# A stack of four graph layers on one core: two PSUM banks in turn for the attention passes' extra sums, and another order of VectorE's work in a step

## The chip, the cores and the metric

The kernel runs on one NeuronCore of a Trainium2 chip. The metric is device time in microseconds (us) of one execution, lower being better. The engines are TensorE (PE), VectorE (DVE), ScalarE (ACT), GpSimd (POOL) and SyncE (SP). Each has its own queue of instructions and works through it in order; they meet at semaphores.

## The reference

There are 3125 nodes with 128 features and 53125 edges, sorted by target node. Four layers are added to x, each on relu(layernorm(x)): a graph attention layer (one head), a relational layer, two graph convolutions with norms, and two transformer convolutions (four heads), the second on the first one's result. The change concerns the attention layers, which are segment softmaxes followed by weighted sums:

```
alpha = sum_d q[dst] * (k[src] + e) / sqrt(C)         # per edge and head
amax  = segment_max(alpha, dst);  p = exp(alpha - amax[dst])
denom = segment_sum(p, dst);      w = p / denom[dst]
out   = segment_sum((v[src] + e) * w, dst) + x @ Ws + bs
```

The kernel divides at the end. So it needs for every node the sum of p times v (the main sums, 128 features) and a few extra sums: of p and of p times the edge weight for each head (8 rows in the transformer layers), and 3 rows in the first layer.

## The kernel before, in words

There are three attention passes, all written by the same Python functions: the first (k = 0) for the graph attention layer, and the second and third (k = 1 and 2, called L3 in the code) for the transformer convolutions. Edges go in tiles of 128, groups of four tiles (512 edges), and chunks of eight groups. A pass has 13 chunks, so 104 groups, and every engine runs a loop over steps s that is unrolled, one group per step and stage:

- POOL gathers the source rows of group s with four indirect DMAs (`attention_gathers`, L518, the gathers are L532) into a ring. The ring has 24 slots in the first pass and 15 in the others. A slot is free once the messages of its old group are made, so POOL waits for `msg_ready`.
- SP loads the query windows of the targets (L436) and the targets' places (L424).
- PE expands the query windows to edges (bank QX, `expand`), and 12 groups later (LAG) sums messages per node (`node_sums`, L1512): it clears bank NU[s % 2] with a matmul of zeros, adds four tiles of messages times one-hot, then clears MTB in the same way and adds four tiles of edge factors times one-hot. It waits for `ex_used` before it clears MTB, which is to say until DVE has taken the previous group's extra sums out of this one bank.
- DVE multiplies queries by keys (`products`), sums by head (`head_sums`, L981), finds the running maximum by scans once in a chunk, scales values to messages (`messages`), and adds PE's sums from PSUM to the sums in SBUF (`add_sums`, L985). Elementwise adds and products of two tensors all show as line L834, a helper.
- ACT makes the one-hot matrices and the exponentials.

The order in a DVE step of the second and third pass is: head sums of s-1, main sums of s-13, extra sums of s-13, first half of messages of s-11, products of s, a part of the chunk's score work (`FIRST`), second half of the messages, another part of the score work (`SECOND`). The first pass has no head sums and no products, and makes its messages in one piece (four instructions, L1008). With r the step's place in its chunk, the score work is at r = 0 (scores, then scans, which need PE's transpose in bank MID), r = 1 (scans over tiles, segment maxima), r = 2 (below the maximum, change of maximum, factors), and r = 4 (the shared node's sums are rescaled with `facs`, L1091 and L1092). PE's own part of it (`turn_scores`, `tile_ends`, `tile_starts`, `turn_maxima`, `spread_changes`, all in bank MID) stands after its `node_sums` at r = 0, 1 and 2. ACT reads columns of MID for `facs` and then signals `fac_ready`.

## Time and profile before

| what | value |
|---|---|
| median of three runs | 4391.96 us (4387.48 to 4392.62) |
| the profiled execution's own time | 4389.91 us |
| its span from first to last instruction | 4387.9 us |
| busy: PE, DVE, ACT, POOL | 2793.6, 2080.7, 1555.9, 2371.9 us |
| first attention pass | from about 250 to 885 us |
| second and third pass | about 2910 to 3550 and 3700 to 4350 us |
| mean granted TensorE clock | 0.772 |

No engine is busy for more than 64% of the span. "Idle before" in a row is the time in which the engine stood still just before the instruction, and the name behind the arrow is what ended it. "Remote" means that a semaphore ended it that the profile can't put down to an instruction that had just finished. A line is often a helper's, so groups are told apart by the names of their tiles: `sums_transposed<-sums_transposed,NU` is the main sum, `extra_sums_transposed<-extra_sums_transposed,MTB` the extra sum, `MTB<-start_penalty,zero_weights` the clearing matmul of the extra sums' bank.

### The profile page before, as it was taken

The numbers are of one execution on the slowest core, as the hardware profiler recorded it, in microseconds if no ns is written. First come the engines' busy times: TensorE is split into PE (matmuls) and PEld (weight loads), VectorE is DVE, ScalarE is ACT, GpSimd is POOL, SyncE is SP. The second block draws the span as 40 slices with busy tenths as digits, with TensorE's granted clock in tenths as the row PEclk, the third lists the DMA queues.
The fourth block names the chain that finished last, engine by engine and source line by source line (L and its number), as shares of the span: only waits on it lengthen the run. The fifth ranks groups of instructions, "written<-read, shape, count | busy, mean of one in ns | idle before, by whom it ended". The sixth has DMA issues, their size and how long they took to land.

```text
span 4387.9 us, 52346 instructions
## 1 busy us (share of the span) xinstructions
PE 2793.6 (64%) x15364; PEld 2036.7 (46%) x15364; DVE 2080.7 (47%) x4427; ACT 1555.9 (35%) x3919; POOL 2371.9 (54%) x2449
## 2 busy tenths in 40 slices
PE   3177788872333356877767877557676774666667
PEld 2055556632222334555534554345555553455555
DVE  5033334641222345566546655235555663555557
ACT  2054444540000033333343333234454423444443
POOL 1745555116666636666366664335666534555653
PEclk9976666885555668899879988567888886887887
DMA  4322222131111112222122221345555424455541
GB/s 86 68 56 59 62 60 62 23 130 47 46 46 48 45 56 53 53 53 53 53 61 55 53 52 34 105 126 141 139 144 146 129 81 128 135 139 135 146 135 45
DMA packets 351656, 360.74 MB, mean 82 GB/s; under 512 B 125198, under 2 KB 274389, under 8 KB 351381
## 3 DMA queue, kind: packets, MB, share of 16 engines
q0 software_dynamic: 89600, 211.77, 18.4%
q1 hardware_dynamic: 255638, 143.69, 12.7%
q10 hardware_dynamic: 6148, 1.93, 0.3%
q8 instruction: 139, 2.28, 0.2%
q14 instruction: 131, 1.07, 0.1%
HBM read 327.08 MB, written 30.26 MB: 81 GB/s over the span
## 4 chain that ended last, share of the span: by engine, by line
PE 41%; another core or an unknown queue 21%; DVE 15%; issue 15%; ACT 3%; POOL 1%; DMA 1%; SPq 1%; DVEq 1%; ACTq 1%; POOLq 0%
PE QX L1368 20%; PE NU L1368 12%; PE MTB L1368 7%; DVE sums_transposed L834 3%; DVE extra_sums_transposed L834 2%; DVE gathered_rows L834 1%; DVE messages L834 1%; DVE query_key_products L834 1%; POOL gathered_rows L549 1%; PE MID L1368 1%; SPq L436 1%; DVE scan_scores L981 1%; ACT window_distance L698 1%; ACTq L601 0%
## 5 line engine op out<-in xcount | busy, mean ns | idle before, releaser
L532 POOL DMA_INDIRECT gathered_rows<-key_value_rows,src_index x832 | 829.6, 997 | 646.2 <-DVE messages L834 356.3
L834 DVE TENSOR_TENSOR sums_transposed<-sums_transposed,NU 128x512 f32 x624 | 425.7, 682 | 1140.7 <-remote 740.6
L549 POOL DMA_INDIRECT gathered_rows<-gcn_rows,src_index x720 | 684.5, 951 | 470.0 <-issue 194.6
L532 POOL DMA_INDIRECT gathered_rows<-gat_rows,src_index x416 | 397.0, 954 | 391.6 <-DVE messages L1008 191.1
L1368 PE MATMUL NU<-start_penalty,zero_weights 128*128 128x512 bf16 x624 | 278.5, 446 | 423.1 <-DVE sums_transposed L834 328.1
L549 POOL DMA_INDIRECT gathered_rows<-relation_rows,src_relation_index x416 | 400.9, 964 | 206.2 <-issue 123.8
L794 ACT ACTIVATE gathered_rows<-iota_window,dst_in_window_by_edge 128x128 f32<-128x128 f32 x832 | 265.1, 389 | 608.4 <-remote 445.0
L729 ACT ACTIVATE edge_node_onehot<-iota_window,dst_in_window_by_edge 128x128 f32<-128x128 f32 x1248 | 394.8, 387 | 155.1 <-remote 135.4
L1368 PEld LDWEIGHTS NU<-edge_node_onehot,messages 128*128 128x128 f32 x2496 | 414.0, 234 | 47.0 <-issue 26.5
L1368 PE MATMUL NU<-gathered_rows 128*128 128x128 f32 x2496 | 395.5, 310 | 56.5 <-issue 33.3
L1368 PE MATMUL NU<-edge_node_onehot,messages 128*128 128x128 f32 x2496 | 413.6, 318 | 24.7 <-issue 24.6
L1368 PEld LDWEIGHTS NU<-gathered_rows 128*128 128x128 f32 x2496 | 386.7, 224 | 85.7 <-issue 66.0
L1368 PE MATMUL MTB<-edge_node_onehot,edge_factors 128*8 128x128 f32 (+1 forms) x2496 | 412.8, 321 | 0.0
L1368 PE MATMUL QX<-query_window,gathered_rows 128*128 128x384 bf16 x1120 | 248.9, 368 | 156.1 <-DVE gathered_rows L834 79.7
L1368 PE MATMUL QX<-query_window,node_edge_onehot 128*128 128x132 f32 (+1 forms) x1248 | 213.3, 313 | 191.7 <-issue 95.8
L834 DVE TENSOR_TENSOR extra_sums_transposed<-extra_sums_transposed,MTB 8x512 f32 (+1 forms) x312 | 210.0, 673 | 256.8 <-remote 183.0
L1368 PEld LDWEIGHTS MTB<-edge_node_onehot,edge_factors 128*8 128x8 f32 (+1 forms) x2496 | 256.1, 103 | 132.1 <-issue 33.5
L698 ACT ACTIVATE window_distance<-dst_in_window_row,minus_partition 128x512 bf16<-128x512 bf16 x312 | 224.2, 718 | 237.9 <-issue 140.4
L1368 PE MATMUL MTB<-start_penalty,zero_weights 128*8 128x512 bf16 x312 | 142.1, 455 | 249.1 <-DVE extra_sums_transposed L834 232.8
L1368 PEld LDWEIGHTS NU<-start_penalty,zero_weights 128*128 128x128 bf16 x624 | 78.4, 126 | 461.3 <-DVE sums_transposed L834 344.9
L709 ACT COPY query_edge_term<-QX 128x16 f32<-128x16 f32 x208 | 38.0, 183 | 717.6 <-DVE query_key_products L834 613.8
L1368 PEld LDWEIGHTS QX<-query_window,node_edge_onehot 128*128 128x128 f32 x1248 | 188.3, 230 | 223.9 <-issue 216.2
(294 smaller groups left out, 4357.0 us busy)
## 6 DMA issues: line engine op xcount, KB each, us to landing
query_window<-query_rows SPq DMA_DIRECT2D x832, 66.0 KB
dst_in_window_row<-dst_in_window SPq DMA_DIRECT2D x156, 256.0 KB
gathered_rows<-key_value_rows,src_index POOLq DMA_INDIRECT x832
relation_rows<-gathered_rows SPq DMA_DIRECT2D x25, 512.0 KB
gathered_rows<-gcn_rows,src_index POOLq DMA_INDIRECT x720
dst_in_window_row<-src_place_and_block SPq DMA_DIRECT2D x28, 256.0 KB
gathered_rows<-gat_rows,src_index POOLq DMA_INDIRECT x416
query_window<-gat_target_scores SPq DMA_DIRECT2D x416, 2.0 KB
```

The lines of the kernel that those rows point to most:

```text
L436: sp.dma_start(qwin[:, s % QS, t, 0:a["ww"]].bitcast(u8), win[ds(bases[t], P * row)].rearrange("(p w) -> p w", w=row)).then_inc(qwin_in[s ...
L532: pool.indirect_dma_start(out=rows_of(a, s)[:, t, :], out_offset=None, in_=a["table"], in_offset=bass.IndirectOffsetOnAxis(ap=srcI[:, TPG ...
L549: pool.indirect_dma_start(out=linear_rows(p["k"], k)[:, t, :], out_offset=None, in_=p["table"], in_offset=bass.IndirectOffsetOnAxis(ap=p[" ...
L698: own.step(act.activation(STa[:, s % 2, :], drow_sb[:, half, q:q + TPG * P], ACT.Square, bias=neg_iota_p[:]))
L709: act.copy(qwe[:, s // GPC % 2, :, TPG * g:TPG * (g + 1)].rearrange("p h t -> p t h"), QX[s % 2][:, :, D:D + HEADS]).then_inc(S["qwe_kept" ...
L729: last = act.activation(to[:, t, :], iota_j[:], ACT.Square, bias=dstP[:, TPG * s + t:TPG * s + t + 1], scale=-1.0)
L794: last = act.activation(to[:, t, :], iota_j[:], ACT.Square, bias=dstP[:, TPG * k + t:TPG * k + t + 1], scale=-1.0)
L834: return dve.tensor_tensor(o, x, y, op)
L981: d.step(dve.tensor_reduce(alphax[:, :, TPG * g:TPG * g + TPG].rearrange("p h t -> p t h"), prod[:, s % 2, :].rearrange("p (t h d) -> p t ...
L1368: return pe.matmul(o, l, r, start=start, stop=stop)
```

## The change

Extra sums go to two PSUM banks. In the first pass they alternate between MTB and the free upper half of QX0. In the other two passes they go to MID where r is 3, 5 or 7, and to MTB where r is 0, 1, 2, 4 or 6. MID is also the bank of the score work, so PE waits for `fac_ready` before it clears MID for extra sums, and `turn_scores` waits until the last extra sums in MID are taken. PE's wait for `ex_used` before it clears a bank now names the last group that used this bank. DVE's extra sums are a function of their own (`add_extras`), called after the second half of the messages and before `SECOND`. The main sums wait for the previous main sums (`nu_used`), and PE waits for `nu_used` before it clears NU. No arithmetic, no transfer and no count of instructions on an engine changes.

```diff
--- before.py
+++ after.py
@@ -334,6 +334,18 @@
         att_base = lambda a: a["k"] * NG
         last_step = NG + LAG + 2
 
+        def ext_bank(k, s):
+
+            if k == 0:
+                return QXf[0][:, 512:1024] if s % 2 else MTB[:]
+            return MID[:] if (s + LAG) % GPC in (3, 5, 7) else MTB[:]
+
+        def ext_before(k, s):
+
+            same = [q for q in range(s) if (s % 2 == q % 2 if k == 0 else
+                                            ((s + LAG) % GPC in (3, 5, 7)) == ((q + LAG) % GPC in (3, 5, 7)))]
+            return same[-1] if same else None
+
         def in_slot(s, ring_size):
             return s // ring_size + 1
 
@@ -990,11 +1002,17 @@
                     dve.wait_ge(S["nu_ready"], b + s + 1)
                     if s % GPC == 0:
                         dve.wait_ge(S["rescaled"], cb + s // GPC + 1)
-                    elif not L3 or s + LAG >= NG:
+                    else:
+                        dve.wait_ge(S["nu_used"], b + s)
+                    tt(numS[:, w], numS[:, w], NU[s % 2][:], ALU.add).then_inc(S["nu_used"], 1)
+
+                def add_extras(s):
+
+                    w = ds(held["base"][s % 4], SPAN)
+                    dve.wait_ge(S["ex_ready"], b + s + 1)
+                    if s:
                         dve.wait_ge(S["ex_used"], b + s)
-                    tt(numS[:, w], numS[:, w], NU[s % 2][:], ALU.add).then_inc(S["nu_used"], 1)
-                    dve.wait_ge(S["ex_ready"], b + s + 1)
-                    tt(extS[0:ex, w], extS[0:ex, w], MTB[0:ex, 0:SPAN], ALU.add).then_inc(S["ex_used"], 1)
+                    tt(extS[0:ex, w], extS[0:ex, w], ext_bank(k, s)[0:ex, 0:SPAN], ALU.add).then_inc(S["ex_used"], 1)
 
                 def messages(s, t0, t1):
                     g = s % GPC
@@ -1107,6 +1125,8 @@
                         FIRST[r](c)
                     if 0 <= s + 1 - LAG < NG:
                         messages(s + 1 - LAG, TPG // 2 if L3 else 0, TPG)
+                    if 0 <= s - 1 - LAG < NG:
+                        add_extras(s - 1 - LAG)
                     if r in SECOND and 0 <= c < NCH:
                         SECOND[r](c)
                 dve.wait_ge(S["ex_used"], b + NG)
@@ -1485,6 +1505,8 @@
                     last.then_inc(S["expand_done"], 1)
 
                 def turn_scores(c):
+                    if L3 and c:
+                        pe.wait_ge(S["ex_used"], b + GPC * c + GPC - LAG)
                     pe.wait_ge(S["alpha_ready"], cb + c + 1)
                     x = (alpha if L3 else alphax)[:].rearrange("p h t -> p (h t)")
                     pe.transpose(MID[:, 0:P], x, I[:]).then_inc(S["xT_ready"], 1)
@@ -1515,15 +1537,20 @@
                     off = offsets(s, f"off_{k}")
                     pe.wait_ge(S["s_ready"], sb0 + s + 1)
                     pe.wait_ge(S["msg_ready"], b + s + 1)
+                    if s >= 2:
+                        pe.wait_ge(S["nu_used"], b + s - 1)
                     clear(NU[s % 2], P)
                     for t in range(TPG):
                         last = mm(NU[s % 2][:, ds(off[t], P)], msg[:, s % 2, t, :], Sb[:, s % SBN, t, :], False, t == TPG - 1)
                     last.then_inc(S["nu_ready"], 1)
-                    if s:
-                        pe.wait_ge(S["ex_used"], b + s)
-                    clear(MTB, 8)
+                    to, before = ext_bank(k, s), ext_before(k, s)
+                    if before is not None:
+                        pe.wait_ge(S["ex_used"], b + before + 1)
+                    if L3 and (s + LAG) % GPC in (3, 5, 7):
+                        pe.wait_ge(S["fac_ready"], cb + min((s + LAG) // GPC, NCH))
+                    clear(to, 8)
                     for t in range(TPG):
-                        last = mm(MTB[0:ex, ds(off[t], P)], pe8[:, c % 2, 0:ex, TPG * g + t], Sb[:, s % SBN, t, :], False, t == TPG - 1)
+                        last = mm(to[0:ex, ds(off[t], P)], pe8[:, c % 2, 0:ex, TPG * g + t], Sb[:, s % SBN, t, :], False, t == TPG - 1)
                     last.then_inc(S["ex_ready"], 1)
 
                 HOPS = {0: (turn_scores, tile_ends), 1: (tile_starts, turn_maxima), 2: (spread_changes,)}
```

DVE, second pass, one step with nothing of the score work (r = 3), before:

```order
L981 TENSOR_REDUCE scan_scores<-query_key_products 128x4x4 [waits k_used]
L834 ISA [waits nu_ready]
L834 TENSOR_TENSOR sums_transposed<-sums_transposed,NU 128x512
L834 REGISTER_ALU [waits ex_ready]
L834 TENSOR_TENSOR extra_sums_transposed<-extra_sums_transposed,MTB 8x512
L834 TENSOR_TENSOR messages<-gathered_rows,edge_factors 128x256
L834 TENSOR_TENSOR query_key_products<-QX,gathered_rows 128x512 [waits gathered13,expand_done]
L834 TENSOR_TENSOR messages<-gathered_rows,edge_factors 128x256
```

The same step of DVE with the change (the helper's line is now L846):

```order
L993 TENSOR_REDUCE scan_scores<-query_key_products 128x4x4 [waits k_used]
L846 ISA [waits nu_used,nu_ready]
L846 TENSOR_TENSOR sums_transposed<-sums_transposed,NU 128x512
L846 TENSOR_TENSOR messages<-gathered_rows,edge_factors 128x256
L846 TENSOR_TENSOR query_key_products<-QX,gathered_rows 128x512 [waits gathered13,expand_done]
L846 TENSOR_TENSOR messages<-gathered_rows,edge_factors 128x256
L846 REGISTER_ALU [waits ex_used,ex_ready]
L846 TENSOR_TENSOR extra_sums_transposed<-extra_sums_transposed,MID 8x512
```

The extra sums and their wait for `ex_ready` have moved behind both halves of the messages and the products.

PE, second pass, the end of one step's main sums and the extra sums behind them, then the chunk's transpose of scores, before:

```order
L1368 MATMUL NU<-edge_node_onehot,messages 128x128
L1368 MATMUL MTB<-start_penalty,zero_weights 8x512 [waits ex_used]
...
L1368 MATMUL NU<-start_penalty,zero_weights 128x512 [waits msg_ready,s_ready]
...
L1368 MATMUL MTB<-start_penalty,zero_weights 8x512 [waits ex_used]
...
L1490 MATMUL MID<-identity,scores 128x128 [waits alpha_ready]
```

The same place of PE with the change (helper's line L1388):

```order
L1388 MATMUL NU<-edge_node_onehot,messages 128x128
L1388 MATMUL MID<-start_penalty,zero_weights 8x512 [waits fac_ready,ex_used]
...
L1388 MATMUL NU<-start_penalty,zero_weights 128x512 [waits nu_used,msg_ready,s_ready]
...
L1388 MATMUL MTB<-start_penalty,zero_weights 8x512 [waits ex_used]
...
L1512 MATMUL MID<-identity,scores 128x128 [waits alpha_ready,ex_used]
```

PE's instructions stand in the same order; every second bank of extra sums is now another one, and the waits name other groups.

## Rows read from the trace of the kernel before

**Rows 1.** Windows: stretch, us, busy (count) per engine, clock, DMA share, GB/s

```profile
250.00:885.00 635.00, 521.79 (x2768) 387.76 (x2768) 274.81 (x892) 310.14 (x731) 302.69 (x319) 0.69 0.26 54
2910.00:3550.00 640.00, 456.29 (x2818) 355.61 (x2819) 372.77 (x858) 319.05 (x834) 356.91 (x356) 0.81 0.47 130
3700.00:4350.00 650.00, 446.12 (x2784) 347.32 (x2784) 370.23 (x847) 317.32 (x831) 359.18 (x356) 0.82 0.47 128
```

**Rows 2.** Waits of POOL in passes one, two, three: us, times, longest

```profile
POOL gathered_rows L532 <- DVE messages L1008: 159.0, 45, 6.1
...
POOL gathered_rows L532 <- DVE messages L834: 134.0, 43, 5.9
...
POOL gathered_rows L532 <- DVE messages L834: 142.0, 36, 7.6
```

**Rows 3.** Groups (lines view), the extra sums on DVE, passes one to three

```profile
L834 DVE TENSOR_TENSOR extra_sums_transposed<-extra_sums_transposed,MTB 3x512 f32 x104 | 70.1, 674 | 134.8 <-remote 91.4 <-PE MTB L1368 43.0
...
L834 DVE TENSOR_TENSOR extra_sums_transposed<-extra_sums_transposed,MTB 8x512 f32 x104 | 69.9, 672 | 53.9 <-remote 42.8 <-PE MTB L1368 6.6 <-issue 4.2
...
L834 DVE TENSOR_TENSOR extra_sums_transposed<-extra_sums_transposed,MTB 8x512 f32 x104 | 69.9, 673 | 68.2 <-remote 48.8 <-issue 9.9 <-PE MTB L1368 9.1
```

**Rows 4.** Groups (lines view), PE clearing the bank of extra sums, passes one to three

```profile
L1368 PE MATMUL MTB<-start_penalty,zero_weights 128*8 128x512 bf16 x104 | 53.7, 516 | 63.5 <-DVE extra_sums_transposed L834 63.5
...
L1368 PE MATMUL MTB<-start_penalty,zero_weights 128*8 128x512 bf16 x104 | 44.3, 426 | 99.1 <-DVE extra_sums_transposed L834 91.6 <-issue 7.5
...
L1368 PE MATMUL MTB<-start_penalty,zero_weights 128*8 128x512 bf16 x104 | 44.0, 423 | 86.4 <-DVE extra_sums_transposed L834 77.7 <-issue 8.7
```

**Rows 5.** Timeline, second pass: start us, us, engine, what, [idle before]

```profile
3099.93 1.05 PE L1368 MATMUL NU<-edge_node_onehot,messages 128*128 128x128 f32 x8
...
3106.36 0.94 POOL L532 DMA_INDIRECT gathered_rows<-key_value_rows,src_index  x1 [0.30 <-issue]
3109.43 0.69 DVE L834 TENSOR_TENSOR sums_transposed<-sums_transposed,NU 128x512 f32 x1 [8.92 <-remote]
3110.03 0.67 DVE L834 TENSOR_TENSOR extra_sums_transposed<-extra_sums_transposed,MTB 8x512 f32 x1
...
3112.08 0.42 DVE L834 TENSOR_TENSOR messages<-gathered_rows,edge_factors 128x256 f32<-128x256 f32 x1
...
3112.77 0.94 POOL L532 DMA_INDIRECT gathered_rows<-key_value_rows,src_index  x1 [5.46 <-DVE messages L834]
```

**Rows 6.** Timeline, second pass, half a chunk later

```profile
3140.85 0.95 POOL L532 DMA_INDIRECT gathered_rows<-key_value_rows,src_index  x1 [0.30 <-issue]
3142.89 0.68 DVE L834 TENSOR_TENSOR extra_sums_transposed<-extra_sums_transposed,MTB 8x512 f32 x1 [2.88 <-remote]
...
3145.10 0.94 POOL L532 DMA_INDIRECT gathered_rows<-key_value_rows,src_index  x1 [3.30 <-DVE messages L834]
```

**Rows 7.** Timeline, first pass

```profile
525.85 0.94 POOL L532 DMA_INDIRECT gathered_rows<-gat_rows,src_index  x1 [0.30 <-issue]
...
528.47 0.68 DVE L834 TENSOR_TENSOR extra_sums_transposed<-extra_sums_transposed,MTB 3x512 f32 x1 [3.60 <-remote]
...
530.19 0.94 POOL L532 DMA_INDIRECT gathered_rows<-gat_rows,src_index  x1 [3.40 <-DVE messages L1008]
```

**Rows 8.** Timeline, second pass, the chunk step with the change of maximum

```profile
3123.25 0.67 DVE L834 TENSOR_TENSOR extra_sums_transposed<-extra_sums_transposed,MTB 8x512 f32 x1
...
3124.47 0.38 PE L1368 MATMUL MTB<-start_penalty,zero_weights 128*8 128x512 bf16 x1
...
3125.56 0.41 DVE L834 TENSOR_TENSOR messages<-gathered_rows,edge_factors 128x256 f32<-128x256 f32 x1
...
3126.55 0.14 ACT L719 ACTIVATE rescale_factors<-MID 8x1 f32<-8x1 f32 x1
...
3128.75 0.38 PE L1368 MATMUL MTB<-start_penalty,zero_weights 128*8 128x512 bf16 x1 [0.40 <-issue]
...
3130.49 0.67 DVE L834 TENSOR_TENSOR sums_transposed<-sums_transposed,NU 128x512 f32 x1
```

## The prediction

> **What bounds the kernel now.** I began with the waits of each engine, went on to the windows of the three attention passes, then to the groups of lines inside them, and last to the timeline of single steps.
>
> The windows say how much of the kernel the change can touch. The passes take 635, 640 and 650 us, together 1925 us, or 6.11, 6.15 and 6.25 us for each of 104 groups. Nothing else is edited. In none of them is an engine busy all the time, PE being nearest with 522 of 635 us in the first pass [rows 1].
>
> The nearest thing to a floor is POOL. Each group costs it four gathers, and in a run of gathers one row reads 0.94 us with 0.30 us of idle time before it [rows 5]. Four times 1.24 us is 4.96 us a group, 516 us a pass. What POOL takes beyond that is mostly time in which it waits for a ring slot, that is for DVE's messages: 159.0, 134.0 and 142.0 us, in 45, 43 and 36 waits [rows 2]. These 435.0 us in 124 waits are what can be won in all. A faster PE or DVE helps only so far as it shortens them.
>
> The timeline shows what such a wait is made of. DVE stands still for 8.92 us before a main sum. PE's matmuls for that sum ended at 3100.98, but DVE goes on only at 3109.43, 2.1 us after POOL's last gather ended at 3107.30. POOL stood because its ring was full. Then DVE takes its main sum, the extra sum and the messages, and POOL starts again at 3112.77, after 5.46 us [rows 5]. So DVE's long stops do not end when PE is done. They end when the stream of gathers pauses, and the ring is refilled only when DVE has reached the end of the messages.
>
> Two spots have a second stop between the main sum and the extra sum. DVE has the rows and factors for the next messages, but the extra sum stands ahead of them in its queue and waits for PE's result: 2.88 us in one spot [rows 6] and 3.60 us in another [rows 7].
>
> **Part 1: the extra sum leaves the way to the messages.** The extra sum begins 0.60 us after the main sum, which is listed with 0.69 us, and is listed itself with 0.67 us [rows 5]. Adds of this size follow each other 0.60 us apart, so that is what one of them costs. With the change it stands behind the messages. In each of POOL's 124 waits for messages the slot is free 0.60 us sooner: 124 x 0.60 = 74 us.
>
> **Part 2: the stop before the extra sum leaves the way to the messages too.** DVE stood 134.8, 53.9 and 68.2 us before extra sums, 256.9 us in all [rows 3]. Not all of it cost POOL anything, since it was still gathering in part of it. In one spot the last gather ended at 3141.80 and the extra sum began at 3142.89, so POOL stood in 1.09 of 2.88 us [rows 6]. In the other it ended at 526.79 and the extra sum began at 528.47: 1.68 of 3.60 us [rows 7]. Together that is 2.77 of 6.48 us, or 43%. Taken over all, 0.43 x 256.9 = 110 us.
>
> **Part 3: the second bank.** PE stood 63.5, 91.6 and 77.7 us before it could clear the bank of extra sums, because DVE had not taken the last ones [rows 4]. With two banks it clears the other one and goes on to the next query windows and main sums. I cost this at nothing in the sum: in rows 5 PE had ended long before DVE was let go. It does keep part 2 from coming back, because a delayed extra sum no longer holds PE. Without it, moving the extra sums later would hold PE longer.
>
> **Part 4: what is given back.** No work disappears. DVE does the same 0.60 us in the same step, and the stop before the extra sum moves behind the messages, where it holds up the next step. Also, POOL now goes on gathering where it used to pause. By rows 5 to 7 a stop of DVE lasts until the gathers pause, so a stop that used to end at 3142.89 will now last through four more gathers, some 5 us, before POOL runs out of slots. Then there is one pause for the two that there were, with its own restart. The bounds are that all comes back (0) or nothing does (74 + 110 = 184 us). I see no row that puts it nearer to one end, because the restart itself (main sum, messages) stays, while the number of restarts should fall. I take half, 92 us.
>
> A rule speaks for the upper end. "SBUF — State Buffer" of the Trainium skill, under "Who interferes with whom", says that DMA never contends with a compute engine and that PE never waits on anyone. By that, the stops that end as the gathers pause are coincidence, nothing would be given back, and the sum would be the full 184 us. The three stops in rows 5 to 7, ending 2.1, 1.1 and 1.7 us after the last gather, speak against it.
>
> **Part 5: the new waits.** The waits for `nu_used` name sums that were done a step earlier in the same queue, so they cost nothing. The wait for `fac_ready` at r = 3 has room: ACT's last factor is done at 3126.69, and PE clears its bank for the next extra sums at 3128.75 [rows 8], 2.1 us later. At r = 1 and r = 2 the banks do not alternate in the second and third pass. There PE waits for an extra sum that has moved behind the products, the score work and the messages. In rows 8 it would end about where the messages end, at 3125.97, and PE cleared the bank at 3124.47. So PE is 1.5 us late once in a chunk. Its main sums were then needed about 2 us after they were ready (the extra sum's bank is cleared at 3128.75, right behind them, and DVE takes the main sum at 3130.49), so this is hidden. Without that slack it costs 1.5 us x 26 chunks = 39 us.
>
> **Sum.** 4389.9 - 92 = 4298 us for the profiled execution. The median of the runs is 2 us above that execution, so I say 4300 us.
>
> **Rivals.**
>
> *All is given back.* The stop only changes its place, POOL pauses as long in all as before, and the time stays at 4392, within 9 us. For it speaks that the sum over a chunk of what DVE must do is unchanged and that its stops follow the gathers. Against it speaks that POOL has more slots open when DVE stops. Chance 0.12.
>
> *Nothing is given back.* 4390 - 184 = 4206, with the median 4208 us. This is what the rule named above would make of it. Chance 0.15. It would show as stops of DVE that end with PE's matmuls.
>
> *Slower: PE's late extra sums at r = 1 and 2 become the bound.* The place is PE's queue in the second and third pass. It is in order, so a bank cleared late delays the change of maximum, the next query windows and the next main sums behind it. The price is 1.5 us for each of 26 chunks, or 39 us. Where POOL's longer stream also draws out DVE's stops so that parts 1 and 2 come to nothing, the time is 4392 + 39 = 4431 us. It decides once PE's lead over DVE falls under 1.5 us at r = 3; in rows 8 it is about 2. Chance 0.16.
>
> *The change doesn't do what it says* can be left out: the order of the two queues shows the move, and there is no scheduler between.
>
> **How the numbers follow.** The forecast (half kept) has 0.57, full gain 0.15, no change 0.12, slower 0.16. About 0.2%, 9 us, is what a measurement of this kernel can tell from no change. Faster is 0.57 + 0.15 = 0.72, the same 0.12, slower 0.16. The range takes in the forecast, most of the full gain and the unchanged time: 4215 to 4400 us. Left out are the slower case and a little of the far end. The likeliest case alone would be 4240 to 4360 us.
>
> **What would show it.** If the steps are right, POOL's waits for messages in the three passes fall from 435 us to about 340, and in number below 124. PE's waits of 233 us before clearing a bank of extra sums fall to under 100. DVE's idle time moves from before the extra sums to before the main sums, and some stops grow longer than the 8.92 us of rows 5. The passes together take about 1830 us instead of 1925, and nothing changes outside them. Part 4 is wrong if DVE's stops end with PE's matmuls; part 5 is wrong if DVE begins to wait for PE's main sums or factors at r = 3 or 4. The prediction fails as a whole if POOL waits as long as before.

## Result and profile after

| | before | changed |
|---|---|---|
| median of four runs each, same chip | 4390.61 us (4387.48 to 4392.62) | 4439.74 us (4433.54 to 4442.13) |
| profiled execution, its span | 4389.91, 4387.9 us | 4438.21, 4436.2 us |
| busy: PE, DVE, ACT, POOL | 2793.6, 2080.7, 1555.9, 2371.9 us | 2779.1, 2072.8, 1558.2, 2334.9 us |

The ratio is 1.0124, 95% interval 1.0104 to 1.0143: 49 us slower, where 92 us less was forecast. No engine does more work, so the 49 us are waits.

The three passes in the windows of the changed kernel (us, then busy time and count of PE, PEld, DVE, ACT, POOL, clock, DMA share, GB/s):

```profile
250.00:885.00 635.00, 489.94 (x2774) 366.98 (x2775) 272.04 (x893) 310.46 (x732) 302.02 (x319) 0.74 0.26 54
2907.00:3580.00 673.00, 466.10 (x2814) 358.43 (x2814) 370.04 (x854) 320.38 (x834) 341.19 (x356) 0.81 0.45 124
3730.00:4400.00 670.00, 462.30 (x2807) 354.78 (x2807) 368.76 (x849) 317.90 (x830) 341.38 (x356) 0.81 0.45 124
```

From the first to the last main sum, by the timelines, the first pass takes 628 us where it took 630, the second 658 where it took 624, the third 655 where it took 641. So the first pass is unchanged and the other two give 34 + 14 = 48 us. DVE's and ACT's busy times answer to [rows 1] within 3 us. PE's is 32 us lower in the first pass, where its granted clock was 0.74 instead of 0.69, and 10 and 16 us higher in the other two; POOL's is 16 and 18 us lower in those two.

POOL's waits for DVE's messages, to be held against [rows 2] (the columns are us, times, longest). One window a pass; the second one takes in the wait of 41.8 us with which the pass begins:

```profile
POOL gathered_rows L544 <- DVE messages L1026: 157.4, 37, 7.1
...
POOL gathered_rows L544 <- DVE messages L846: 218.3, 44, 41.8
...
POOL gathered_rows L544 <- DVE messages L846: 176.3, 43, 7.1
```

That is 157.4 + (218.3 - 41.8) + 176.3 = 510.2 us in 37 + 43 + 43 = 123 waits, against 435.0 us in 124. Their number has not fallen, and the mean wait is longer, 4.1 us against 3.5.

Where DVE stands, second pass, groups of the lines view with the idle time before them. First the kernel before (its extra sums are in [rows 3]):

```profile
L834 DVE TENSOR_TENSOR sums_transposed<-sums_transposed,NU 128x512 f32 x104 | 70.6, 679 | 154.4 <-remote 100.5 <-PE NU L1368 38.8 <-issue 14.9
...
L1034 DVE TENSOR_TENSOR_SCAN forward_max<-start_penalty,MID 128x128 f32<-128x128 bf16 x12 | 5.0, 420 | 19.1 <-PE MID L1490 10.4 <-issue 8.7
...
L1054 DVE SCALAR_TENSOR_TENSOR segment_max<-start_seen_penalty,MID,forward_max 128x128 f32<-128x128 bf16 x12 | 4.3, 356 | 25.8 <-issue 15.0 <-PE MID L1368 10.8
```

Then the changed kernel:

```profile
L846 DVE TENSOR_TENSOR sums_transposed<-sums_transposed,NU 128x512 f32 x104 | 70.5, 678 | 129.7 <-remote 108.1 <-PE NU L1388 20.9 <-DVE extra_sums_transposed L1110 0.4
...
L846 DVE TENSOR_TENSOR extra_sums_transposed<-extra_sums_transposed,MTB 8x512 f32 x65 | 43.5, 670 | 1.5 <-issue 0.8 <-PE MTB L1388 0.7
L846 DVE TENSOR_TENSOR extra_sums_transposed<-extra_sums_transposed,MID 8x512 f32 x39 | 26.2, 671 | 61.1 <-remote 49.3 <-issue 7.9 <-PE MTB L1388 3.5
L1052 DVE TENSOR_TENSOR_SCAN forward_max<-start_penalty,MID 128x128 f32<-128x128 bf16 x12 | 5.0, 420 | 71.9 <-remote 67.8 <-issue 3.4 <-PE MID L1512 0.6
...
L1072 DVE SCALAR_TENSOR_TENSOR segment_max<-start_seen_penalty,MID,forward_max 128x128 f32<-128x128 bf16 x12 | 4.3, 361 | 27.5 <-issue 19.5 <-PE MID L1388 8.1
```

The stop before the extra sums, 53.9 us in [rows 3], is now 1.5 + 61.1 = 62.6 us. The stops before the main sums fell by 25 us. In the first pass the idle time before extra sums did fall, from 134.8 to 71.8 us, but it came back before the main sums (144.4 to 169.1 us) and the scans (25.1 to 64.1 us). In the second pass DVE stands 71.9 us before the scans instead of 19.1, in the third 73.9 instead of 34.5. PE's waits before it clears a bank of extra sums, 233 us in [rows 4], are nearly gone; the one bank where they are left, in the second and the third pass:

```profile
L1388 PE MATMUL MTB<-start_penalty,zero_weights 128*8 128x512 bf16 x65 | 25.9, 398 | 23.1 <-DVE extra_sums_transposed L846 18.7 <-issue 4.3
...
L1388 PE MATMUL MTB<-start_penalty,zero_weights 128*8 128x512 bf16 x65 | 25.8, 396 | 24.6 <-DVE extra_sums_transposed L846 18.9 <-issue 5.6
```

A chunk of the second pass in the timeline of the changed kernel (start us, us, engine, what, idle before it), in the three places where DVE stands long:

```profile
3193.72 0.95 POOL L544 DMA_INDIRECT gathered_rows<-key_value_rows,src_index  x1 [0.30 <-issue]
...
3196.45 0.69 DVE L846 TENSOR_TENSOR sums_transposed<-sums_transposed,NU 128x512 f32 x1 [7.15 <-remote]
...
3198.68 0.94 POOL L544 DMA_INDIRECT gathered_rows<-key_value_rows,src_index  x1 [4.01 <-DVE messages L846]
...
3202.95 0.45 PE L1388 MATMUL MID<-start_penalty,zero_weights 128*8 128x512 bf16 x1
...
3203.24 1.04 PE L1388 MATMUL MID<-edge_node_onehot,edge_factors 128*8 128x128 f32 x8
...
3212.48 0.94 POOL L544 DMA_INDIRECT gathered_rows<-key_value_rows,src_index  x1 [0.30 <-issue]
...
3215.05 0.68 DVE L846 TENSOR_TENSOR extra_sums_transposed<-extra_sums_transposed,MID 8x512 f32 x1 [9.95 <-remote]
...
3218.46 0.95 POOL L544 DMA_INDIRECT gathered_rows<-key_value_rows,src_index  x1 [5.03 <-DVE messages L846]
...
3221.69 0.67 DVE L846 TENSOR_TENSOR extra_sums_transposed<-extra_sums_transposed,MID 8x512 f32 x1
...
3223.91 0.33 PE L1512 MATMUL MID<-identity,scores 128*128 128x128 f32 x1
...
3227.26 0.95 POOL L544 DMA_INDIRECT gathered_rows<-key_value_rows,src_index  x1 [0.30 <-issue]
3229.90 0.42 DVE L1052 TENSOR_TENSOR_SCAN forward_max<-start_penalty,MID 128x128 f32<-128x128 bf16 x1 [7.54 <-remote]
...
3234.81 0.94 POOL L544 DMA_INDIRECT gathered_rows<-key_value_rows,src_index  x1 [6.61 <-DVE messages L846]
```

DVE stands 7.15 us before a main sum, 9.95 us before an extra sum and 7.54 us before the scans. The extra sum's matmuls in MID ended at 3204.28, before DVE even began to stand at 3205.10, so DVE was let go 10.8 us after PE had finished. The scans need PE's transpose, which ends at 3224.24, yet DVE goes on at 3229.90. POOL's last gather had ended at 3194.67, 3213.42 and 3228.21. Each stop ends 1.6 to 1.8 us after that, much as in [rows 5] (2.1 us). In the whole of the second and third pass 23 and 28 stops of DVE were longer than 4 us before (156 and 188 us), and 33 and 35 are now (224 and 228 us), counted in the two timelines. In the changed kernel the median of these 68 ends 1.7 us after POOL's last gather.

Not every stop fits this picture, and the prediction's sentence that they end when the stream of gathers pauses is too general. Of the 51 long stops before the change, 22 end inside a run of gathers, most of them 12 to 15 us after the run began; of the 68 after it, 11 do. One of the 22, in the kernel before:

```profile
2976.03 2.10 PE L1368 MATMUL QX<-query_window,relation_weights 128*128 128x132 f32 x8 [3.17 <-issue]
...
2978.35 1.51 PE L1368 MATMUL NU<-edge_node_onehot,messages 128*128 128x128 f32 x8
2978.98 0.95 POOL L532 DMA_INDIRECT gathered_rows<-key_value_rows,src_index  x1 [0.30 <-issue]
2980.14 0.69 DVE L834 TENSOR_TENSOR sums_transposed<-sums_transposed,NU 128x512 f32 x1 [6.89 <-PE NU L1368]
2980.23 0.95 POOL L532 DMA_INDIRECT gathered_rows<-key_value_rows,src_index  x1 [0.30 <-issue]
```

Here PE itself stood 3.17 us without a cause that the profile shows, and DVE went on 0.28 us after PE's end, with POOL gathering all the while. Nor is every wait of DVE on PE drawn out: of the 128 main sums in the three passes before which DVE waited, it began 60 within 1 us of PE's end and 47 more than 4 us after it.

### The profile page after: what moved, and what is told of

The parts are those of the page before. It is cut to its first block, busy times and chain, and to the rows that moved or that the text cites. A ratio compares the mean times of both kernels' runs of the same rounds, so it can differ in the third digit from the quotient of the medians.

```text
span 4436.2 us, 52915 instructions
## 1 busy us (share of the span) xinstructions
PE 2779.1 (63%) x15364; PEld 2019.9 (46%) x15364; DVE 2072.8 (47%) x4427; ACT 1558.2 (35%) x3919; POOL 2334.9 (53%) x2449
## 4 chain that ended last, share of the span: by engine, by line
PE 37%; another core or an unknown queue 24%; DVE 16%; issue 15%; ACT 3%; DMA 1%; SPq 1%; DVEq 1%; ACTq 1%; POOL 0%; POOLq 0%
PE QX L1388 20%; PE NU L1388 11%; DVE sums_transposed L846 3%; PE MTB L1388 3%; DVE query_key_products L846 2%; DVE messages L846 2%; PE MID L1388 2%; DVE extra_sums_transposed L846 2%; DVE gathered_rows L846 2%; DVE scan_scores L993 1%; SPq L448 1%; ACT window_distance L710 1%; DVE messages L1026 1%; ACTq L613 0%
## 5 line engine op out<-in xcount | busy, mean ns | idle before, releaser
L544 POOL DMA_INDIRECT gathered_rows<-key_value_rows,src_index x832 | 796.1, 957 | 719.0 <-DVE messages L846 431.7
L846 DVE TENSOR_TENSOR sums_transposed<-sums_transposed,NU 128x512 f32 x624 | 425.3, 682 | 1160.5 <-remote 816.6
L1388 PE MATMUL NU<-start_penalty,zero_weights 128*128 128x512 bf16 x624 | 276.6, 443 | 452.3 <-DVE sums_transposed L846 329.4
L1388 PE MATMUL NU<-edge_node_onehot,messages 128*128 128x128 f32 x2496 | 422.7, 320 | 45.3 <-issue 44.6
L1388 PEld LDWEIGHTS NU<-edge_node_onehot,messages 128*128 128x128 f32 x2496 | 415.7, 234 | 75.4 <-issue 56.3
L1388 PE MATMUL NU<-gathered_rows 128*128 128x128 f32 x2496 | 388.8, 307 | 51.8 <-issue 34.1
L1388 PEld LDWEIGHTS NU<-gathered_rows 128*128 128x128 f32 x2496 | 381.1, 221 | 79.7 <-issue 63.0
L1388 PE MATMUL QX<-query_window,node_edge_onehot 128*128 128x132 f32 (+1 forms) x1248 | 228.4, 316 | 290.8 <-issue 236.5
L1388 PEld LDWEIGHTS QX<-query_window,node_edge_onehot 128*128 128x128 f32 x1248 | 196.5, 232 | 320.3 <-issue 310.0
L1388 PE MATMUL QX<-query_window,gathered_rows 128*128 128x384 bf16 x1120 | 249.5, 372 | 138.9 <-DVE gathered_rows L846 74.5
L1388 PEld LDWEIGHTS NU<-start_penalty,zero_weights 128*128 128x128 bf16 x624 | 76.1, 122 | 497.1 <-DVE sums_transposed L846 344.9
L721 ACT COPY query_edge_term<-QX 128x16 f32<-128x16 f32 x208 | 37.6, 181 | 644.4 <-DVE query_key_products L846 542.5
L1388 PE MATMUL MTB<-edge_node_onehot,edge_factors 128*8 128x128 f32 (+1 forms) x1456 | 229.9, 301 | 50.4 <-issue 48.4
L1388 PEld LDWEIGHTS QX<-query_window,gathered_rows 128*128 128x128 bf16 x1120 | 116.7, 108 | 236.2 <-issue 122.5
L1388 PE MATMUL QX<-query_window,relation_weights 128*128 128x132 f32 x832 | 169.1, 365 | 60.4 <-issue 35.6
```

The source lines that it names most:

```text
L544: pool.indirect_dma_start(out=rows_of(a, s)[:, t, :], out_offset=None, in_=a["table"], in_offset=bass.IndirectOffsetOnAxis(ap=srcI[:, TPG ...
L721: act.copy(qwe[:, s // GPC % 2, :, TPG * g:TPG * (g + 1)].rearrange("p h t -> p t h"), QX[s % 2][:, :, D:D + HEADS]).then_inc(S["qwe_kept" ...
L846: return dve.tensor_tensor(o, x, y, op)
L1388: return pe.matmul(o, l, r, start=start, stop=stop)
```

## The experiments

**What the theories say.** Theory A: on this chip, while POOL streams gathers, a wait of DVE on PE isn't let go when PE is done but when the gathers have drained (given the counts above it can hold for a part of the waits only). The new order has the messages first, so POOL streams again before DVE reaches its waits on PE, and there are more of them under the stream. The rivals put the cost on the second bank and its waits, or on PE being late, and take the stops' ends for chance.

**Parts of the change alone.** The first three variants: all extra sums in MTB, with DVE's new order and neither of the two new waits of PE that go with MID; both banks, with the old order; the change in the first pass alone.

```diff
 # order only
         def ext_bank(k, s):
-            if k == 0:
-                return QXf[0][:, 512:1024] if s % 2 else MTB[:]
-            return MID[:] if (s + LAG) % GPC in (3, 5, 7) else MTB[:]
+            return MTB[:]
...
-                    if L3 and (s + LAG) % GPC in (3, 5, 7):
-                        pe.wait_ge(S["fac_ready"], cb + min((s + LAG) // GPC, NCH))
...
-                    if L3 and c:
-                        pe.wait_ge(S["ex_used"], b + GPC * c + GPC - LAG)
 # banks only
                     if 0 <= s - 1 - LAG < NG:
                         add_sums(s - 1 - LAG)
+                        add_extras(s - 1 - LAG)
...
-                    if 0 <= s - 1 - LAG < NG:
-                        add_extras(s - 1 - LAG)
```

> The change without its second bank: extra sums stand behind the messages on DVE, and all go to MTB. Theory A (the new place of the extra sums makes DVE reach PE's answers while POOL streams gathers, and each such meeting becomes a long stop; three in a chunk instead of two): the order is what costs, so 4430 to 4450 us, near the changed kernel's 4440, with a stop of some 7 us before the scans of line forward_max in each chunk of the second and third pass. Theory B (PE is held by late extra sums, my recorded rival): with one bank PE is held in every step and not only at r = 1 and 2, so clearly slower than the changed kernel, 4460 to 4520 us, and the first pass is longer than its 630 us too.

> The change without its order: two banks in turn as in the change, but the extra sums stand right behind the main sums as before. Theory A: DVE's stops stay where they were before the change, two in a chunk, so the time is that of the kernel before within 15 us (4375 to 4405). Theory B: PE is held less than before, so faster, 4340 to 4380. A third reading (the wait for fac_ready and MID in turn with the score work are what costs) expects 4430 or more.

> The change in the first pass alone (its order and its second bank); the second and third pass as before. By the trace of the changed kernel the first pass is 2 us shorter and the others 48 us longer, so both theories expect 4385 to 4392 us. If it is above 4400, the passes are not independent, and what the first pass leaves (ring, semaphores, clock) costs the later ones.

Measured on one chip, and a different one: the kernel before took **3611.79 us** there, not 4391. The order alone took 3575.53 us, ratio 0.9905 (0.9891 to 0.9919); the banks alone 3613.32 us, 1.0003 (0.9993 to 1.0013); the first pass alone 3602.80 us, 0.9977 (0.9964 to 0.9991). So on this chip the new order makes the kernel faster. The long stops are nearly absent. In the second and third pass the order-only kernel has 8 and 2 stops over 4 us, the banks-only kernel none. The difference is plain in the first linear pass, whose code no variant touches. On the chip of the first comparison (kernel before):

```profile
1200.42 1.92 PE L1368 MATMUL NU<-gathered_rows 128*128 128x128 f32 x8
...
1204.18 0.95 POOL L549 DMA_INDIRECT gathered_rows<-relation_rows,src_relation_index  x1 [0.30 <-issue]
1207.72 0.69 DVE L834 TENSOR_TENSOR sums_transposed<-sums_transposed,NU 128x512 f32 x1 [7.16 <-remote]
1207.86 0.94 POOL L549 DMA_INDIRECT gathered_rows<-relation_rows,src_relation_index  x1 [2.73 <-remote]
```

and on the other chip (the banks-only kernel):

```profile
1002.05 2.04 PE L1387 MATMUL NU<-gathered_rows 128*128 128x128 f32 x8 [2.54 <-DMA gathered_rows<-relation_rows,src_relation_index]
1003.15 0.94 POOL L561 DMA_INDIRECT gathered_rows<-relation_rows,src_relation_index  x1 [0.30 <-issue]
...
1004.23 0.69 DVE L846 TENSOR_TENSOR sums_transposed<-sums_transposed,NU 128x512 f32 x1 [3.72 <-PE NU L1387]
1004.40 0.95 POOL L561 DMA_INDIRECT gathered_rows<-relation_rows,src_relation_index  x1 [0.30 <-issue]
```

Above, PE is done at 1202.34 and DVE goes on at 1207.72, after POOL's gathers have paused; POOL's own wait of 2.73 us there ends at the same moment. Below, PE is done at 1004.09, DVE goes on at 1004.23, and POOL streams through it. A gather takes POOL 0.95 us in both. These three runs are a result on that kind of chip only. The others below say which kind they had.

**Half of the gathers.** In the second and third pass two of the four gathers of each group are left out, so these kernels compute with old rows for half of the edges there:

```diff
-                    for t in range(TPG):
+                    for t in range(TPG // 2 if a["k"] else 0, TPG):
                         pool.indirect_dma_start(
```

> The kernel before, with two of the four gathers of each group left out in the second and third pass (the rows of the other two tiles are then what the ring last held, so the outputs are not the reference's). POOL needs some 2.5 us a group there instead of 5. Theory A (DVE's long stops last until the stream of gathers pauses): the two stops of 5 to 10 us in each chunk shrink to under 3 us, and the two passes take 400 to 520 us each instead of 640 and 650. Theory B (the round trips between PE and DVE bound the passes, gathers do not matter): the passes keep over 600 us each.

> The changed kernel with the same gathers left out. Theory A: the third stop is gone with the stream, and the new order costs nothing or gains: within 15 us of the kernel before with half its gathers, or faster than it. Theory B: PE is held by the late extra sums as before, so it is slower than that kernel by 40 us or more, as with all gathers.

Measured, before at 4381.21 us: 3979.24 us, ratio 0.9084 (0.9055 to 0.9113), and 3964.48 us, 0.9045 (0.9016 to 0.9073). With half of the gathers the changed kernel leads by 15 us instead of trailing by 49. Its second and third pass take 463 and 455 us, those of the kernel before 488 and 444. The penalty needs the full stream. That fits theory A, but so would any cause that comes with POOL being busy.

**The whole change and its parts on one chip, before at 4426.05 us.**

> The changed kernel itself, so that the runs beside it have it on the same chip. Chips differ: the kernel before took 4391 and 4381 us on some, 3612 us on the one where the first three variants ran. Theory A (a wait of VectorE on TensorE that falls into a stream of gathers is drawn out to the stream's pause; the change adds such a wait at the scans): where the kernel before takes about 4390 us the ratio is 1.010 to 1.014 again; where it takes about 3612 us such long stops are nearly absent, and the changed kernel is as fast as the order-only variant or a little faster, ratio 0.985 to 0.992. Theory B (the changed kernel is slower for a reason of its own, such as the shared bank MID): slower on either kind of chip, ratio above 1.005.

> VectorE's new order alone: extra sums behind the messages, all in MTB, and no wait of the transpose of scores for the extra sums. It was at 0.9905 where the kernel before took 3612 us. Theory A: on a chip where before takes about 4390 us, the third stop (before the scans) is shorter than in the changed kernel, since the transpose no longer waits for the extra sum of the same step, but the two others stay: ratio 1.000 to 1.008, below that of the changed kernel by 0.003 to 0.012. Theory B' (the new order by itself is what costs there): the same ratio as the changed kernel, 1.010 to 1.014. Theory C (the bank is what costs): below 1, near 0.99, on either chip.

> Two banks alone: the extra sums stay right behind the main sums. It was at 1.0003 where the kernel before took 3612 us. Theory A: VectorE's order is that of before, so its stops are too, two in a chunk; ratio 0.997 to 1.003 on either chip. Theory C (the bank, with its waits for fac_ready and ex_used, is what costs): above 1.006 on a chip where before takes about 4390 us.

The last of the four has the extra sums of r = 7 in MTB:

```diff
-            return MID[:] if (s + LAG) % GPC in (3, 5, 7) else MTB[:]
+            return MID[:] if (s + LAG) % GPC in (3, 5) else MTB[:]
...
-                        pe.wait_ge(S["ex_used"], b + GPC * c + GPC - LAG)
+                        pe.wait_ge(S["ex_used"], b + GPC * c + GPC - LAG - 2)
```

> The changed kernel with the extra sums of r = 7 in MTB instead of MID, so that the transpose of scores at r = 0 waits for an extra sum two steps older (that of r = 5) and no longer for the one that VectorE takes in the same step just before its scans. Theory A with its sharper form (that wait makes a round trip from VectorE to TensorE and back, just before the scans, and it is this that is drawn out: 6.0 and 6.2 us on average before the scans where before had 1.6 and 2.9): the stop before the scans falls to 3 us or less in the second and third pass, and the ratio is 0.005 to 0.01 below that of the changed kernel. Rival (the stop stands before the scans because the gathers stream there, whatever the transpose waits for): the idle time before the scans stays at 5 to 6 us and the ratio is within 0.002 of the changed kernel's.

| kernel | median us | ratio (95%) | second, third pass | idle before the scans |
|---|---|---|---|---|
| changed | 4491.55 | 1.0148 (1.0125 to 1.0172) | 683, 671 us | 80.5, 71.8 us |
| order only | 4519.49 | 1.0220 (1.0187 to 1.0253) | 694, 688 us | 37.2, 38.5 us |
| banks only | 4444.29 | 1.0030 (1.0012 to 1.0049) | 656, 662 us | 20.0, 15.7 us |
| r = 7 in MTB | 4493.76 | 1.0141 (1.0118 to 1.0165) | 689, 680 us | 82.6, 73.7 us |

The order is what costs, and the banks win back a third of it. With the old order the banks cost a little themselves: 1.0030 is at the edge of the 0.997 to 1.003 that theory A gave. My expectation for the order alone, 1.000 to 1.008, was wrong. Its stop before the scans is shorter, but DVE stands at more places of a chunk (main sums at r = 4, 6 and 0, extra sums at r = 0), and in all 332 us in the second pass against 323. The sharper form of theory A fell too: with r = 7 in MTB the transpose no longer waits for an extra sum of the same step, and the stop before the scans stays. This is its row in that kernel, second pass:

```profile
L1052 DVE TENSOR_TENSOR_SCAN forward_max<-start_penalty,MID 128x128 f32<-128x128 bf16 x13 | 5.5, 421 | 83.1 <-remote 81.0 <-PE MID L1512 2.1
```

So the new wait of the transpose doesn't make the third stop. The two rows of the table with a shorter stop before the scans stand longer at other sums; that a stop stands where DVE first needs PE while POOL streams is my reading of this, and no run isolates it.

**A pause in the gathers.** This tests the part that the gathers play. Nothing is taken away; POOL gets one more wait. Before every second group it waits until its last group has landed:

```diff
                     if s >= slots:
                         pool.wait_ge(S["msg_ready"], att_base(a) + s - slots + 1)
+                    if s and s % 2 == 0:
+                        pool.wait_ge(gathered[(s - 1) % slots], landed(a["k"], s - 1))
```

> The changed kernel, and GpSimd waits before every second group of an attention pass until its last group of gathers has landed, so that no run of gathers is longer than two groups (some 10 us), with a pause of about 2 us behind it. The computation is complete. Floor of GpSimd: (2 x 4.96 + 2) / 2 = 6.0 us a group, under the 6.1 to 6.5 that the passes take. Theory A (on chips where before takes about 4390 us, VectorE's waits on TensorE are drawn out until the stream of gathers has drained): the stops before the main sums, the extra sums and the scans fall from 6 to 7 us to 3 or 4, and the ratio falls from 1.012 to 1.015 to below 1.00, at best 0.98. Rival (the stops have a cause of their own, and GpSimd only happens to be idle when they end): stops keep their length, GpSimd has less lead, and the time is that of the changed kernel or up to 2% more, ratio 1.012 to 1.035. Where before takes about 3612 us there are hardly any long stops: by either theory GpSimd, at 6.0 us a group against 4.8, becomes the bound, ratio near 1.08.

> The kernel before with the same pause after every second group in the attention passes. Theory A: its stops are shortened too; ratio below 1.00, at best 0.98, and the distance to the changed kernel with the pause is under 0.005, either way, because what the change adds to the stops is gone. Rival: ratio 1.00 to 1.02, and the changed kernel with the pause stays 0.01 or more above it.

> The changed kernel with the pause after every group: a run of gathers is at most 5 us long. GpSimd's floor is then 4.96 + 2 = 7.0 us a group, above what the passes take now, so the time is expected longer by either theory: 3 passes x 104 x (7.0 - 6.3) = 218 us more, ratio about 1.05 to 1.06. What tells the theories apart is VectorE's stops: by theory A none of those at the main sums and the scans is longer than about 5 us, and they no longer stand at fixed steps of the chunk but wherever GpSimd is late; by the rival stops of 6 to 7 us remain before the scans and the main sums of r = 4.

Measured, before at 4382.16 us: changed kernel with the pause **4197.06 us, ratio 0.9574 (0.9554 to 0.9594)**; kernel before with the pause 4201.09 us, 0.9569 (0.9542 to 0.9596); pause after every group 4614.53 us, 1.0512 (1.0489 to 1.0536). The first two are 181 to 185 us faster than before, which is more than theory A allowed (at best 0.98), and there is no difference between them. With the pause after every group GpSimd's pace is the bound, passes of 714, 759 and 761 us, and DVE waits for gathered rows before its products instead of standing at main sums and scans, as both theories' prices said. In the changed kernel with the pause, second pass, POOL's own waits for its landings are

```profile
POOL gathered_rows L546 <- DMA gathered_rows<-key_value_rows,src_index: 129.8, 45, 4.5
```

and DVE's stops are

```profile
L848 DVE TENSOR_TENSOR sums_transposed<-sums_transposed,NU 128x512 f32 x103 | 69.8, 677 | 105.6 <-remote 85.2 <-PE NU L1390 19.7 <-DVE extra_sums_transposed L1112 0.4
...
L848 DVE TENSOR_TENSOR extra_sums_transposed<-extra_sums_transposed,MID 8x512 f32 x39 | 26.2, 672 | 19.0 <-remote 18.3 <-PE MID L1390 0.7
...
L1054 DVE TENSOR_TENSOR_SCAN forward_max<-start_penalty,MID 128x128 f32<-128x128 bf16 x12 | 5.0, 421 | 8.4 <-PE MID L1514 7.8 <-issue 0.6
...
L1074 DVE SCALAR_TENSOR_TENSOR segment_max<-start_seen_penalty,MID,forward_max 128x128 f32<-128x128 bf16 x12 | 4.3, 356 | 68.4 <-remote 62.8 <-PE MID L1390 5.6
```

Before the scans 8.4 us are left of 71.9, before the extra sums in MID 19.0 of 61.1, before the main sums 105.6 of 129.7 (the control below, from the same chip as this trace, has 79.0, 80.2 and 112.2). The stop before the segment maxima has grown from 27.5 to 68.4, so part of it only moved, and 53 stops over 4 us (303 us) are left in the second and third pass, 11 of them waits for gathered rows. POOL's waits for messages, 176.5 us in the second pass of the changed kernel, are down to

```profile
POOL gathered_rows L546 <- DVE messages L848: 0.9, 3, 0.3
```

and its own pauses of 129.8 us stand in their place. The pass takes 621 us against 658.

The kernel before, with the pause, shows more of it. Second pass:

```profile
L836 DVE TENSOR_TENSOR sums_transposed<-sums_transposed,NU 128x512 f32 x104 | 70.2, 675 | 8.1 <-remote 6.5 <-PE NU L1370 1.3 <-DVE extra_sums_transposed L1094 0.2
...
L836 DVE TENSOR_TENSOR query_key_products<-QX,gathered_rows 128x512 f32<-128x512 f32 x91 | 62.2, 683 | 171.1 <-DMA gathered_rows<-key_value_rows,src_index 167.6 <-issue 3.5
```

Of 154.4 us before main sums 8.1 are left, but DVE now waits 171 us for gathered rows. Its passes take 606, 621 and 625 us, those of the changed kernel 600, 621 and 621. That is 5.97 us a group in the second pass of either, which is the floor of 6.0 us that the expectation gave for POOL with its pauses. So the two kernels are equal at a point where POOL's pace bounds both, and their equality doesn't show by itself that the pause removes what the new order adds; the comparison with half of the gathers, where the changed kernel leads, has no such floor.

**Controls.** The same wait, but for the landing of the group before the last one (nothing has to drain); the pause only while the ring is first filled; the pause in the linear passes too, before every fourth group; and before every third group.

```diff
 # wait without a pause
+                    if s >= 2 and s % 2 == 0:
+                        pool.wait_ge(gathered[(s - 2) % slots], landed(a["k"], s - 2))
 # pause in the fills: the pause above, only if 0 < s < slots
 # linear too: the pause above, and in the linear passes
+                    if q and q % 4 == 0:
+                        pool.wait_ge(lgathered[(q - 1) % LRING], 16 * TPG * ((q - 1) // LRING + 1))
 # every third group
+                    if s and s % 3 == 0:
```

> A control: the changed kernel, GpSimd waits before every second group of an attention pass as in e10, but for the landing of the group before the last one, whose last gather ended at least 5 us ago. Nothing has to drain. If the draining is what helped in e10: the ratio is that of the changed kernel, 1.010 to 1.015. If a wait in itself helps: about 0.957 as e10. A third way: if the landing's signal reaches GpSimd late too while gathers stream, this wait makes a pause by itself, as far as the signal is held, and the ratio lies between the two.

> The changed kernel with the pause of e10 only while the ring is first filled (24 groups in the first pass, 15 in the others), none in the steady part. In e10 the stretch up to the first main sum fell from 254 to 189 us, those before the second and third pass from 194 to 155 and from 165 to 128: 141 us in all, and the passes from 1941 to 1842 us. Theory A: the 141 us come back, the passes stay at about 1941 us with their long stops: 4438 - 141 = 4297 us where before is at 4390, ratio 0.978 to 0.982. Rival (what the pause changes is the phase of the whole pipeline, and it lasts): ratio near 0.957.

> As e10, and in the three linear passes a pause before every fourth group that is gathered. The linear passes take 581, 508 and 517 us where before takes 4388, and 510, 435 and 435 us where it takes 3612; GpSimd's floor with the pause is 4 x 1.24 + 2 / 4 = 5.5 us a group for the first (567 us) and less for the others, some of whose groups are not gathered. Theory A, taken as a matter of the stream and not of the attention passes: the second and third linear pass fall to 450 to 480 us, the first to 565 to 575: 80 to 120 us less than e10, ratio 0.93 to 0.94. Rival (it is bound to the attention passes' round trips): the linear passes get longer by the pauses, 0 to 50 us, ratio 0.957 to 0.97.

> The changed kernel with the pause before every third group. Runs of gathers are up to 15 us long, as long as the ring of the second and third pass has free slots (3 groups) when VectorE stops, so theory A expects their stops to be near those of the changed kernel (6 us), passes of 640 to 660 us, and a gain mostly in the fills: ratio 0.97 to 0.985. If only the number of pauses mattered, the gain would be two thirds of e10's: 1.012 - 0.67 x 0.055 = 0.975, within the same band; the stops in the trace tell more than the time. If GpSimd's pace was e10's limit, it is faster than e10: below 0.955.

These four met a chip of the other kind again (before at 3604.05 us): 3563.20 us, ratio 0.9884 (0.9860 to 0.9908); 3620.21 us, 1.0042 (1.0025 to 1.0059); 4104.91 us, 1.1387 (1.1358 to 1.1416); 3838.31 us, 1.0642 (1.0615 to 1.0669). The first is in effect the changed kernel, since its new waits stop POOL for 8.4 us of the first and 2.4 us of the second pass: on such a chip the change wins 41 us, and DVE has no stop over 4 us in the second and third pass. Its row for the scans there:

```profile
L1054 DVE TENSOR_TENSOR_SCAN forward_max<-start_penalty,MID 128x128 f32<-128x128 bf16 x13 | 5.5, 420 | 12.1 <-PE MID L1514 12.1
```

The pauses only cost there. Two of the four were run once more and met the first kind (before at 4382.66 us).

> The kernel of e15_pause_linear_too once more, for a chip where before takes 4380 to 4430 us; where before took 3604 us it had a ratio of 1.1387, with linear passes of 567, 488 and 493 us, which is what GpSimd's pauses cost there. Theory A, as a matter of the stream: such long linear passes too, since GpSimd's pace is then the bound on either kind of chip, 567 + 488 + 493 = 1548 us against 1606 of before, so 40 to 60 us less than e10, ratio 0.943 to 0.949. Rival (bound to the attention passes' round trips): linear passes at or above those of before, ratio 0.957 or more. On a chip of the faster kind: 1.13 to 1.14 again.

> The kernel of e13_wait_no_pause once more, for a chip where before takes 4380 to 4430 us: GpSimd waits before every second group for the landing of the group before the last one. Where before took 3604 us these waits stopped GpSimd in 11 us of the first pass and 2 us of the second. If draining is what helped in e10: ratio 1.010 to 1.015, that of the changed kernel. If a wait in itself helps: near 0.957. If the landing's signal reaches GpSimd late while it streams: in between, with idle time of GpSimd put down to the gathers' landing. On a chip of the faster kind: 0.986 to 0.991 again.

Wait without a pause: 4447.33 us, ratio 1.0148 (1.0114 to 1.0182), just the changed kernel's. On this chip the scans' row of the second pass reads

```profile
L1054 DVE TENSOR_TENSOR_SCAN forward_max<-start_penalty,MID 128x128 f32<-128x128 bf16 x12 | 5.0, 420 | 79.0 <-remote 78.3 <-PE MID L1514 0.6
```

So a wait that doesn't stop POOL changes nothing, and it is the pause that helps. Whether it helps because the gathers have landed, or only because POOL issues none for some 3 us (129.8 us in 45 waits), these runs don't tell apart. Linear passes too: 4238.21 us, 0.9653 (0.9619 to 0.9686), 41 us more than with the pause in the attention passes alone. The linear passes took 584, 537 and 535 us against 578, 511 and 516. So the pauses help in the attention passes and their fills only, and theory A as a statement about any stream of gathers isn't borne out.

Where the 252 us between the last control (span 4445.3) and the changed kernel with the pause (4193.0) are, stage by stage from the first and last main sums of their timelines:

| stage | wait only | pause | less by |
|---|---|---|---|
| up to the first pass's first main sum | 258 | 189 | 69 |
| first pass | 629 | 600 | 29 |
| ahead of the second pass | 191 | 155 | 36 |
| second pass | 668 | 621 | 47 |
| ahead of the third pass | 160 | 128 | 32 |
| third pass | 659 | 621 | 38 |

More than half, 137 us, comes from the stretches in which POOL fills its ring of 15 to 24 groups in one go. The change doesn't touch them. In the kernel before the share is larger: its traces without and with the pause differ by 185 us (they are from two chips of this kind), of which 140 lie in these three stretches and 44 in the passes. The waits before the first pass show what happens in such a stretch, here in the kernel before, from 150 to 254 us:

```profile
DVE query_edge_term L834 <- PE QX L1368: 102.8, 1, 102.8
...
PE QX L1368 <- issue: 46.3, 4, 12.7
```

DVE stands 102.8 us for PE, and PE itself stands up to 12.7 us at a time without a cause that the profile shows. With the pause the same wait of DVE takes 32.4 us.

## Why the prediction was wrong

The forecast was 4300 us with a range of 4215 to 4400; the time is 4439.74.

- **What bounds the kernel** was read rightly. The observation that DVE's stops end when the gathers pause, not when PE is done [rows 5], is what everything turned on. It holds for 29 of the 51 long stops; the prediction read it from three spots. The pause experiment shows that the gathers play a part in the stops.
- **Part 1 and part 2** (74 + 110 us) counted what leaves the way to the messages. The direction was right where long stops are absent: on the other kind of chip the second and third pass take 489 and 495 us in the changed kernel (the control whose wait hardly stops POOL), and 518 and 522 in the banks-only one. These 56 us are a third of 184, and the runs don't split them between the two parts. On the chip of the forecast, POOL's restarts did not come 0.60 us sooner in sum; POOL waited 510 us instead of 435. Part 2's share of 43% came from two stops, taken for all.
- **Part 4 is the step that failed.** It said "there is one pause for the two that there were" and put the bounds at nothing or all given back. More than all came back. In the old order one drained pause paid for three things: main sum, extra sum and messages came in a row, and PE's results for the sums were there while POOL stood. In the new order the messages come first, POOL starts again at once, and DVE's next waits on PE (extra sum, scans) fall under a fresh stream and last until that one has drained. That succession is read from the timelines and not tested by itself. What the runs show is that the order alone costs 2.2% and the banks alone 0.3%, that the cost is gone with half of the gathers, and that long stops of DVE went from 51 to 68. I had written that a stop "will now last through four more gathers", and then not asked at which other waits of DVE this would happen. Counted in the second and third pass, the idle time before main sums is 262 us instead of 281, before extra sums 122 us as before, and before scans 146 us instead of 54.
- **Part 3** was right in kind: PE's waits for a bank fell from 233 us to 37.6. It isn't worth nothing, though. With the new order the banks bring 1.0220 down to 1.0148; with the old order they cost 0.3%.
- **Part 5** was right that the new waits are mostly hidden. PE never waits long before it clears MID, and at MTB it waits 18.7 + 18.9 us in all.
- **The rivals.** The slower one gave 4431 us, near the time measured, by a mechanism that the trace doesn't bear out as the main one. PE did wait at MTB (18.7 + 18.9 us, against a price of 39), but DVE stood less than 2 us in the second pass before main sums of r = 1 to 3, where PE's lateness would be felt first. Whether it helps to bring on the stop that now stands at r = 4 and stood at r = 5 before wasn't tried. The rival also named the other half of what happened, that parts 1 and 2 come to nothing because the longer stream draws out DVE's stops. That half deserved to be a case of its own, without PE.
- **The rule of the Trainium skill.** "SBUF — State Buffer" of the Trainium skill, under "Who interferes with whom", says that DMA never contends with a compute engine and that PE never waits on anyone. That section is about ports of SBUF, and the instructions' own times give no sign against it: a sum of DVE takes 0.68 us and most gathers 0.95 us on either kind of chip. What the prediction drew from it, that gathers have nothing to do with when DVE's stops end, is what the runs speak against on this kind of chip: two waits of POOL that differ only in the landing they name give 0.9574, where POOL stops, and 1.0148, where it doesn't. On the other kind nothing seen here contradicts it.
- **What would show it.** POOL's waits were to fall to 340 us and below 124 in number: 510 us, 123. PE's bank waits to under 100: yes. Nothing outside the passes changes: yes. The text said that it fails as a whole if POOL waits as long as before, and that is how it failed.

What stays open is why DVE is let go late while gathers are in flight on some chips and not on others. The traces narrow it down. "Remote" stops over 2 us in the kernel before are 337, and 333 of them wait for a semaphore that PE raises: 185 of DVE, 102 of ACT, 46 of POOL. In the seven traces from the other kind of chip there is none. In the stop of [rows 5] the four signals that PE owed, for two main sums, the extra sums and the expanded queries, come one after another between 3109.30 and 3109.61, though the first of them belongs to matmuls that ended at 3100.98 by the profile. So it is PE's side that is late, either its signals or PE itself, whose ends the profile only models: PE's own gaps over 0.8 us with no cause shown add up to 117 us in the second and third pass before, 200 us after, and 67 us in the control on the other kind. Fetches of instructions don't explain it. In these passes a packet of the two instruction queues starts in, or within 1 us before, fewer than half of the stops over 4 us (11 of 23 and 14 of 28 before the change), and the 54 and 52 packets of these two windows would by chance hit half of them. Why the linear passes take 581, 508 and 517 us on one kind of chip and 510, 435 and 435 us on the other, and yet gain nothing from pauses, isn't explained either.

## What to carry to other kernels

When a stop in a trace ends with another engine's pause and not with its own producer's end, count the waits that will fall under the stream after a reordering, not only those that leave the path; to hand work to the streaming engine earlier can lengthen every later wait. Test such a reading by putting a pause in, not only by taking work away: here one added wait made either kernel 4.3% faster. Then look at what bounds the kernel with the pause before reading anything from two versions being equal there. And run both versions on more than one chip, since the sign of this change, and of the pause, depends on it.

## What the hardware showed that was not expected

- The same kernel took 4369 to 4447 us on some chips and 3594 to 3624 us in two of the comparisons, with the same time of a single sum (0.68 us) and of most gathers (0.95 us), and other waits.
- On the first kind, DVE began a main sum that it waited for up to 10.1 us after PE's end in the kernel before, and up to 12.6 us in the changed one. In the changed kernel a long stop ends 1.7 us (median) after the last gather. On the second kind, in the control without a pause, all 148 such sums began within 0.7 us of PE's end.
- What comes late on the first kind is PE's side: 333 of 337 "remote" stops over 2 us, of DVE, ACT and POOL alike, wait for PE.
- With a pause of POOL before every second group, the stretch up to the first sum fell from 254 to 189 us, near the 176 to 178 us of the other kind of chip.
